# State-space networks: the gate's network first for all tokens, its exponentials and factor beside the other three, scan factors fetched by halves of the images

## The chip, the cores and the metric

The kernel runs on one core of a Trainium2 chip. The core has a matrix engine (TensorE, PE in the rows), a vector engine (VectorE, DVE), an engine for activation functions (ScalarE, ACT), a general one (GpSimd, POOL), a queue that issues transfers (SyncE, SP), and 16 DMA engines. Each engine works through its own list of instructions in order and is held up by waits on semaphores. The metric is device time in microseconds for one execution of the whole program; lower is better.

## What is computed

A vision tower on 32 images of 3 x 128 x 128. A tokenizer makes 65 tokens of 192 numbers for each image (2080 tokens in all). Two attention blocks follow, a mixture of experts, then a state-space layer, then a gated mixture of experts. The change is in the state-space layer alone. Cut to what matters, it computes, for every image, token by token:

```
def _mlp(x, w1, b1, w2, b2):
    return jax.nn.silu(x @ w1 + b1) @ w2 + b2

A_log = -jnp.abs(_mlp(x, A_w1, A_b1, A_w2, A_b2))       # 16 numbers a token
Bv = _mlp(x, B_w1, B_b1, B_w2, B_b2)                    # 16
Cv = _mlp(x, C_w1, C_b1, C_w2, C_b2)                    # 16
delta = jax.nn.sigmoid(_mlp(x, d_w1, d_b1, d_w2, d_b2)) # 192
dt = jnp.exp(log_dt)

def step(state, inp):
    a, b, c, dlt, u_t = inp
    dA = jnp.exp(a[:, None, :] * dt[None, :, None])
    cur = u_t[:, :, None] * (b[:, None, :] * dt[None, :, None])
    state = (dlt[:, :, None] * state + (1.0 - dlt[:, :, None]) * cur) * dA
    y = jnp.sum(state * c[:, None, :], axis=2) + u_t * D_param
    return (state, y)
```

The hidden layers of A, B and C have 384 units, that of the gate (d) has 192. The kernel doesn't form the sigmoid. It keeps exp(-z) of the gate's output z, called the ratio: the input of the scan is the gain G = ratio times dt times u, and the logarithm of 1 + ratio goes into the exponent of the scan's factor.

## The kernel before, in words

`state_space` has three stages, each a block that all engines enter and leave together: a block ends when the last engine has come to its end.

**The stage of the networks** (names `ssm_mlp_*`). The tokens are normalised and turned into columns `xT` (96 rows, 2 halves). SP loads the weights. Then the tokens are taken in 8 groups of 4 images, 260 columns each. For every group TensorE computes 11 tiles of hidden units (L2024): 9 of 128 rows for A, B and C, and 2 of 96 rows for the gate. Tile n goes to PSUM bank n mod 4, and TensorE may start it once ScalarE has emptied tile n - 4 (the wait of L2021, `s_act` at n - 3). ScalarE empties each with a Silu into `hid` (L2066). One group later follows the second layer, `layer2(g - 1)`: 9 matmuls for B, C and A into bank 4 (L2007) and 4 for the gate into banks 5 and 6 (L2013). ScalarE then empties them in `evacuate2(g - 1)`: B and C into `BC` (L2050), A into `ST` (L2052), the gate's output into `ratio` (L2056).

After the eighth group, VectorE clamps `ratio` (L1985), ScalarE takes its exponential (L2073, two instructions of 96 x 2080, one for each half of the 192 channels), VectorE makes the gain `G` (L1988), and ScalarE writes log(1 + ratio) into `ST` (L2076). SP, at the end of its list, waits for the last group (L1932), writes `BC` to DRAM (`bandc`, L1934), reads it back spread over 128 rows into `brep` and `crep` (L1937), writes `G` to DRAM (`gains`, L1940) and waits until that has landed (L1941). Then the block ends.

**The scan** (names `ssm_scan_*`) has 48 units of 128 rows (8 channels by 16 states) and 1056 columns (16 images of 66 columns): units 0 to 23 for the first half of the images, 24 to 47 for the second. In each unit SP fetches the gains spread over the rows (`grep`, L2113), TensorE makes the exponents from `ST` (L2168), ScalarE their exponential (L2156), VectorE the product with `brep` (L2137) and the scan itself (L2144), GpSimd the product with `crep` (L2127), and TensorE sums over the states (L2181). VectorE and GpSimd wait for both of `brep` and `crep` before the first unit (L2122, L2131).

**The last stage** turns the result back and adds it to the rows.

What sets the order is the code itself: each engine's list is written out by hand, and only semaphores tie them. An activation function needs its table on ScalarE; where the next function is in another one, the compiler puts an `ACT_TABLE_LOAD` ahead of it.

Of the kernel before, what the change touches and what calls it, by code (L numbers as in the profile page):

```python
# [1849 lines left out]
def state_space(nc, name, rows, known, stats, gains, bandc, w, fetch):  # L1850
# [3 lines left out]
    NL1 = 11  # L1854
# [14 lines left out]
    with ExitStack() as ctx:  # L1869
# [8 lines left out]
        s_rep = st.sem("rep")  # L1878
        with ExitStack() as ctx2:  # L1879
# [12 lines left out]
            hid = [s2.sbuf(f"hid{p}", [PARTS, NL1, GROUP]) for p in range(2)]  # L1892
            BC = s2.sbuf("BC", [32 + STATE, COLS])
# [5 lines left out]
            s_w, s_l1, s_act, s_l2, s_e2, s_sc, s_dt, s_c, s_edge, s_one, s_dtr, s_sel, s_exp, s_cl, s_ln, s_gain, s_skip = (  # L1899
                s2.sem(n) for n in ("w", "l1", "act", "l2", "e2", "sc", "dt", "c", "edge", "one", "dtr", "sel", "exp", "cl", "ln", "gain", "skip"))  # L1900
            block = ctx2.enter_context(nc.Block())
            NB2, NL2 = 5, 5
# [4 lines left out]
            def _(sp):  # L1907
# [52 lines left out]
            def _(dve):  # L1960
# [22 lines left out]
                dve.wait_ge(s_e2, NB2 * groups)  # L1983
# [12 lines left out]
            def _(pe):  # L1996
# [5 lines left out]
                def layer2(g):  # L2002
                    pe.wait_ge(s_act, NL1 * (g + 1))
                    wait(pe, s_e2, NB2 * g)
                    for k in range(3):
                        for i, (_, slot, ft) in enumerate(slots):
                            last = nc.tensor.matmul(ps[32 * slot:32 * slot + STATE, 4 * BANK:4 * BANK + GROUP], W2[:, i, k, :], hid[g % 2][:, ft + k, :],  # L2007
                                                    start=(k == 0), stop=(k == 2))
                            if k == 2:
                                last.then_inc(s_l2, 1)  # L2010
                    for mb in range(2):
                        for kb in range(2):
                            last = nc.tensor.matmul(ps[0:HALF, (5 + mb) * BANK:(5 + mb) * BANK + GROUP], W2d[:, kb, HALF * mb:HALF * mb + HALF],  # L2013
                                                    hid[g % 2][0:HALF, 9 + kb, :], start=(kb == 0), stop=(kb == 1))
                        last.then_inc(s_l2, 1)

                for g in range(groups):
                    for ft in range(NL1):
                        c0, rows_ = l1(ft)
                        n = NL1 * g + ft  # L2020
                        wait(pe, s_act, n - 3)  # L2021
                        for kb in range(2):
                            k = HALF + kb
                            last = nc.tensor.matmul(ps[0:rows_, (n % 4) * BANK:(n % 4) * BANK + GROUP], W1[0:k, kb, c0:c0 + rows_],  # L2024
                                                    xT[0:k, kb, GROUP * g:GROUP * g + GROUP], start=(kb == 0), stop=(kb == 1))
                        last.then_inc(s_l1, 1)
                    if g >= 1:
                        layer2(g - 1)
# [3 lines left out]
            def _(act):  # L2032
# [5 lines left out]
                act.wait_ge(s_edge, 4)  # L2038

                def evacuate2(g):  # L2040
# [13 lines left out]
                    for mb in range(2):  # L2054
                        act.wait_ge(s_l2, NL2 * g + 4 + mb)
                        nc.scalar.activation(ratio[:, mb, GROUP * g:GROUP * (g + 1)], ps[0:HALF, (5 + mb) * BANK:(5 + mb) * BANK + GROUP], ACT.Identity,  # L2056
                                             bias=b2d[:, mb:mb + 1]).then_inc(s_e2, 1)

                for g in range(groups):
                    for ft in range(NL1):  # L2060
                        _, rows_ = l1(ft)
                        n = NL1 * g + ft
# [3 lines left out]
                        nc.scalar.activation(hid[g % 2][0:rows_, ft, :], ps[0:rows_, (n % 4) * BANK:(n % 4) * BANK + GROUP],  # L2066
                                             ACT.Silu).then_inc(s_act, 1)
# [6 lines left out]
                for kb in range(2):  # L2074
                    act.wait_ge(s_exp, kb + 1)
                    nc.scalar.activation(tokens(ST[0:HALF, kb, :]), ratio[:, kb, :].rearrange("p (i c) -> p i c", c=SEQ), ACT.Ln, bias=1.0).then_inc(s_ln, 1)  # L2076


        with ExitStack() as ctx2:
# [50 lines left out]
            def _(dve):  # L2130
                dve.wait_ge(s_rep, 32)  # L2131

                def inputs(n):
                    _, _, cols = unit(n)
# [791 lines left out]
```

## Time and profile before

| | us |
|---|---|
| median of 3 runs | 1965.28 |
| lowest and highest | 1960.82, 1969.39 |
| the profiled execution, its own time | 1966.56 |
| its span in the trace | 1964.8 |
| TensorE busy | 1634.4 (83%) |
| VectorE busy | 1070.3 (54%) |
| ScalarE busy | 774.4 (39%) |
| GpSimd busy | 737.5 (38%) |
| mean granted clock of TensorE | 0.893 of full speed |
| the networks' first matmul | at 1414.1 |
| the scan's first matmul | at 1542.9 |
| the last stage's first matmul | at 1729.6 |

Times inside the trace count from the start of the span. The stage of the networks takes about 129 us of matmuls and tail, the scan about 187 us. The granted clock has two levels: 1.0 is 2.4 GHz and 0.5 is 1.2 GHz. A busy share over the whole span says little on a change of this kind: what counts is which engine is waited for in the networks' stage, and what ends last at its border to the scan.

### The profile page before, as it was taken

Reading aid. Unit: us, or ns where it says so; the run is one execution under the profiler, and the core shown is the slowest. Engines: PE = TensorE matmul, PEld = TensorE weight load, DVE = VectorE, ACT = ScalarE, POOL = GpSimd, SP = SyncE. Lnnn points to the kernel's source line nnn. Section 1 sums busy time; section 2 is a strip of 40 time slices with the busy share of each in tenths; the row PEclk is TensorE's granted clock in tenths of the full one; section 3 lists DMA queues with packets and bytes.
Section 4 is the critical chain, followed back from the end, with each engine's and each line's share of the span. In section 5 each row is a group of like instructions: output and inputs, shape, how many; then the busy total and the mean of one; then the engine's idle time right before and its main releaser. Section 6 shows DMA issues by size and latency. Waiting matters only on the chain. (4 is left out here: it accounts for less than half of the span.)

```text
span 1964.8 us, 34671 instructions
## 1 busy us (share of the span) xinstructions
PE 1634.4 (83%) x11223; PEld 1272.7 (65%) x11224; DVE 1070.3 (54%) x3226; ACT 774.4 (39%) x1433; POOL 737.5 (38%) x680
## 2 busy tenths in 40 slices
PE   3889999959999948887988889996399477767997
PEld 2657777748888834775677879996276233366564
DVE  2678988856667514387276512121700599942332
ACT  0557777723555521372254421111355332324100
POOL 2556767621222204142433023332200399920232
PEclk9989999979999958797988779998599699957999
DMA  3244343323333122000000645552600766534110
GB/s 64 41 94 83 71 81 78 74 65 94 112 109 110 42 67 62 1 3 13 1 2 18 178 122 148 156 157 62 137 1 0 182 158 160 143 87 128 41 47 28
DMA packets 219419, 158.14 MB, mean 80 GB/s; under 512 B 116583, under 2 KB 196404, under 8 KB 218794
## 3 DMA queue, kind: packets, MB, share of 16 engines
q1 hardware_dynamic: 206405, 141.18, 29.2%
q0 software_dynamic: 6528, 14.19, 2.5%
q10 hardware_dynamic: 6374, 1.33, 0.4%
q8 instruction: 64, 1.05, 0.2%
q14 instruction: 48, 0.39, 0.1%
HBM read 106.05 MB, written 32.35 MB: 70 GB/s over the span
## 5 line engine op out<-in xcount | busy, mean ns | idle before, releaser
L2127 POOL TENSOR_TENSOR ssm_scan_prod<-ssm_scan_S,ssm_crep 128x1056 f32<-128x1056 f32 x48 | 159.4, 3320 | 146.0 <-DVE ssm_scan_S L2144 146.0
L1259 PE MATMUL a_psum<-a2w_W,a_hT 128*128 128x256 f32 (+1 forms) x640 | 150.9, 383 | 5.4 <-DVE a_z L1060 4.5
L755 PE MATMUL a_psum<-a_W,a_hT 126*128 126x256 f32 x512 | 135.6, 398 | 0.0
L1259 PEld LDWEIGHTS a_psum<-a2w_W,a_hT 128*128 128x128 f32 (+1 forms) x640 | 119.9, 192 | 21.2 <-issue 6.6
L2168 PE MATMUL ssm_scan_psum<-ssm_ST,ssm_EW 112*128 112x512 f32 (+1 forms) x288 | 106.8, 509 | 23.9 <-PEq L1879 21.3
L2698 PE MATMUL moe_tiles_psum<-moe_tiles_XT,moe_tiles_mine 96*128 96x128 f32 x960 | 119.1, 281 | 2.0 <-DMA moe_tiles_mine<-moe_W 2.0
L2698 PEld LDWEIGHTS moe_tiles_psum<-moe_tiles_XT,moe_tiles_mine 96*128 96x128 f32 x960 | 113.3, 195 | 5.1 <-DMA moe_tiles_mine<-moe_W 2.5
L2144 DVE TENSOR_TENSOR_SCAN ssm_scan_S<-ssm_scan_X,ssm_scan_psum 128x1056 f32<-128x1056 f32 x48 | 113.0, 2354 | 4.7 <-ACT ssm_scan_psum L2156 0.4
L2168 PEld LDWEIGHTS ssm_scan_psum<-ssm_ST,ssm_EW 112*128 112x128 f32 x288 | 52.8, 197 | 92.8 <-issue 71.6
L755 PEld LDWEIGHTS a_psum<-a_W,a_hT 126*128 126x128 f32 x512 | 91.3, 193 | 30.8 <-issue 21.8
L543 POOL TENSOR_TENSOR a_rstd<-a_rstd,a_mhalf 128x8 f32<-128x8 f32 x64 | 105.2, 1643 | 5.0
L2745 ACT ACTIVATE moe_tiles_GT<-moe_tiles_psum 128x512 f32<-128x512 f32 x80 | 39.1, 491 | 161.7 <-PE moe_tiles_psum L2698 123.4
L2790 DVE TENSOR_TENSOR moe_tiles_Y<-moe_tiles_psum,moe_B 128x192 f32<-128x192 f32 x40 | 14.3, 358 | 157.4 <-PE moe_tiles_psum L2682 157.4
L2156 ACT ACTIVATE ssm_scan_psum<-ssm_scan_psum 128x1056 f32<-128x1056 f32 x48 | 49.7, 1035 | 120.7 <-PE ssm_scan_psum L2168 120.7
L2725 PE MATMUL glu_tiles_psum<-glu_W,glu_tiles_XT 96*128 x192 | 84.3, 583 | 6.4 <-DVE glu_tiles_XT L2775 5.5
L2653 POOL DMA_INDIRECT ys<-moe_tiles_Y,moe_target x40 | 39.6, 990 | 129.9 <-DVE moe_tiles_Y L2790 123.6
L2682 PE MATMUL moe_tiles_psum<-moe_W,moe_tiles_GT 128*128 x480 | 84.5, 326 | 0.0
L2024 PE MATMUL ssm_mlp_psum<-ssm_mlp_xT,ssm_mlp_W 96*128 96x260 f32 (+3 forms) x352 | 80.7, 389 | 2.6 <-SPq L1930 2.6
L1017 POOL TENSOR_TENSOR a_yb<-a_y,a2w_b 128x256 f32<-128x256 f32 x16 | 11.6, 726 | 179.6 <-DVE a_O L1106 167.8
L563 POOL TENSOR_TENSOR a_yb<-a_y,a_b 128x512 f32<-128x512 f32 x32 | 40.8, 1276 | 96.9 <-DVE a_O L638 96.9
L2682 PEld LDWEIGHTS moe_tiles_psum<-moe_W,moe_tiles_GT 128*128 128x128 f32 x480 | 77.1, 190 | 0.0
L2024 PEld LDWEIGHTS ssm_mlp_psum<-ssm_mlp_xT,ssm_mlp_W 96*128 96x128 f32 (+3 forms) x352 | 66.2, 188 | 16.0 <-issue 2.9
(640 smaller groups left out, 3906.6 us busy)
## 6 DMA issues: line engine op xcount, KB each, us to landing
ssm_scan_grep<-gains SPq DMA_DIRECT2D x48, 528.0 KB, 4.7
moe_tiles_mine<-moe_W SPq DMA_DIRECT2D x40, 576.0 KB
a2w_X<-t SPq DMA_DIRECT2D x192, 96.0 KB
t<-a_O SPq DMA_DIRECT2D x128, 64.0 KB
xrows<-in_x SPq DMA_DIRECT2D x30, 192.0 KB
a_X<-xrows SPq DMA_DIRECT2D x60, 91.9 KB, 3.0
a_PX<-t SPq DMA_DIRECT2D x96, 48.0 KB
moe_raw_first<-in_L_ffn_w SPq DMA_DIRECT2D x8, 576.0 KB
```

Of the source, the lines that this page charges most:

```text
L543: nc.gpsimd.tensor_tensor(out[:], out[:], mhalf[:], ALU.pow).then_inc(s[done], 1)
L563: nc.gpsimd.tensor_tensor(yb[:], y[:], spread(b2[:], 1, tiles), ALU.add).then_inc(s["yb"], 1)
L755: last = nc.tensor.matmul(KQ[q][:, j, :], hT[0:MAIN, q, PARTS * j:PARTS * j + PARTS], W[0:MAIN, :], start=False, stop=True)
L1259: last = nc.tensor.matmul(KQ[:, j, :], hT[i % 2][0:rows, k, PARTS * j:PARTS * j + PARTS], W[0:rows, k, :], start=(k == 0), stop=(k == 4))
L2024: last = nc.tensor.matmul(ps[0:rows_, (n % 4) * BANK:(n % 4) * BANK + GROUP], W1[0:k, kb, c0:c0 + rows_], xT[0:k, kb, GROUP * g:GROUP * g ...
L2127: nc.gpsimd.tensor_tensor(prod[n % 2][:], S[n % 2][:], crep[:, cols], ALU.mult).then_inc(s_prod, 1)
L2144: nc.vector.tensor_tensor_scan(S[n % 2][:], X[n % 2][:], E[n % 2], 0.0, ALU.add, ALU.mult).then_inc(s_scan, 1)
L2156: nc.scalar.activation(E[n % 2], E[n % 2], ACT.Exp).then_inc(s_coef, 1)
L2168: last = nc.tensor.matmul(E[n % 2][:, a:b], EW[:, j, :], ST[:, j // (NCH // 2), HCOLS * h + a:HCOLS * h + b], start=True, stop=True)
L2682: last = nc.tensor.matmul(made(p), GT[p][0:w_, f, :], W2[0:w_, f, bass.ds(e, 1), :].rearrange("p a c -> p (a c)"), start=(f == 0), stop=(f ...
L2698: last = nc.tensor.matmul(hidT(1 - p, f, 1), mine[q][0:HALF + kb, kb, PARTS * f:PARTS * f + PARTS], XT[1 - p][0:HALF + kb, kb, :], start=( ...
L2725: last = nc.tensor.matmul(hid(c), XT[p][0:k, kb, :], W1[0:k, kb, bass.ds(e, 1), cut * c:cut * c + cut].rearrange("p a c -> p (a c)"), star ...
```

## The change

The gate's network is taken out of the groups. TensorE and ScalarE first go through all 8 groups with the gate's 2 hidden tiles alone, in buffers of their own (`hidd`), with the gate's second layer one group behind (`layer2d`, `evacuate2d`); its last call comes after the second tile of the main loop. The main loop has 9 tiles in a group instead of 11, and a second layer without the gate. VectorE clamps and forms `G` while the main loop runs. ScalarE does the two exponentials behind groups 1 and 2 of the main loop and the two logarithms behind groups 4 and 5 (`BEHIND`), between the emptying of one group's second layer and the first Silu of the next group. SP writes `gains` first, and then `bandc`, `brep` and `crep` in two halves of the images, the first when groups 0 to 3 are done. The waits of VectorE and GpSimd in the scan are made for each half. The number of matmuls, of activations and of bytes moved is as before.

```diff
-    NL1 = 11
+    NL1 = 9
...
+            BEHIND = {1: ("exp", 0), 2: ("exp", 1), 4: ("ln", 0), 5: ("ln", 1)}
...
-                sp.wait_ge(s_e2, NB2 * groups)
-                for i in range(2):
-                    sp.dma_start(dram(bandc, i * STATE * COLS, [(COLS, STATE), (1, COLS)]), BC[32 * i:32 * i + STATE, :]).then_inc(s_sc, 16)
-                sp.wait_ge(s_sc, 32)
-                for i, rep in enumerate((brep, crep)):
-                    sp.dma_start(rep[:], dram(bandc, i * STATE * COLS, [(COLS, STATE), (0, 8), (1, COLS)])).then_inc(s_rep, 16)
                 for kb in range(2):
                     sp.wait_ge(s_gain, kb + 1)
-                    sp.dma_start(dram(gains, kb * HALF * COLS, [(COLS, HALF), (1, COLS)]), G[:, kb, :]).then_inc(s_sc, 16)
-                sp.wait_ge(s_sc, 64)
+                    sp.dma_start(dram(gains, kb * HALF * COLS, [(COLS, HALF), (1, COLS)]), G[:, kb, :]).then_inc(s_gs, 16)
+                for h in range(2):
+                    sp.wait_ge(s_e2, NB2 * (groups // 2) * (h + 1))
+                    for i in range(2):
+                        sp.dma_start(dram(bandc, i * STATE * COLS + HCOLS * h, [(COLS, STATE), (1, HCOLS)]),
+                                     BC[32 * i:32 * i + STATE, HCOLS * h:HCOLS * h + HCOLS]).then_inc(s_sc, 16)
+                    sp.wait_ge(s_sc, 32 * (h + 1))
+                    for i, rep in enumerate((brep, crep)):
+                        sp.dma_start(rep[:, HCOLS * h:HCOLS * h + HCOLS],
+                                     dram(bandc, i * STATE * COLS + HCOLS * h, [(COLS, STATE), (0, 8), (1, HCOLS)])).then_inc(s_rep[h], 16)
+                sp.wait_ge(s_gs, 32)
...
+                def layer2d(g):
+                    pe.wait_ge(s_act, 2 * (g + 1))
+                    wait(pe, s_ed, NLD * g)
...
+                for g in range(groups):
+                    for j in range(2):
+                        first(2 * g + j, g, NL1 + j)
+                    if g >= 1:
+                        layer2d(g - 1)
                 for g in range(groups):
                     for ft in range(NL1):
...
+                        first(2 * groups + NL1 * g + ft, g, ft)
+                        if g == 0 and ft == 1:
+                            layer2d(groups - 1)
                     if g >= 1:
                         layer2(g - 1)
...
+                def exponential(kb):
+                    act.wait_ge(s_cl, kb + 1)
+                    nc.scalar.activation(ratio[:, kb, :], ratio[:, kb, :], ACT.Exp, scale=-1.0).then_inc(s_exp, 1)
+
+                def logarithm(kb):
+                    act.wait_ge(s_exp, kb + 1)
+                    nc.scalar.activation(tokens(ST[0:HALF, kb, :]), ratio[:, kb, :].rearrange("p (i c) -> p i c", c=SEQ), ACT.Ln, bias=1.0).then_inc(s_ln, 1)
...
                     if g >= 1:
                         evacuate2(g - 1)
+                    if g in BEHIND:
+                        kind, kb = BEHIND[g]
+                        (exponential if kind == "exp" else logarithm)(kb)
                 evacuate2(groups - 1)
-                for kb in range(2):
-                    act.wait_ge(s_cl, kb + 1)
-                    nc.scalar.activation(ratio[:, kb, :], ratio[:, kb, :], ACT.Exp, scale=-1.0).then_inc(s_exp, 1)
-                for kb in range(2):
-                    act.wait_ge(s_exp, kb + 1)
-                    nc.scalar.activation(tokens(ST[0:HALF, kb, :]), ratio[:, kb, :].rearrange("p (i c) -> p i c", c=SEQ), ACT.Ln, bias=1.0).then_inc(s_ln, 1)
...
-                pool.wait_ge(s_rep, 32)
                 for n in range(UNITS):
-                    _, _, cols = unit(n)
+                    h, j, cols = unit(n)
+                    if j == 0:
+                        pool.wait_ge(s_rep[h], 32)
```

ScalarE's list at the end of the networks' stage, before: the last group's outputs, then the exponentials and the logarithms, each pair with one table load.

```order
L2050 ACTIVATE ssm_mlp_BC<-ssm_mlp_psum,ssm_mlp_b 16x4x65 x2
L2052 ACTIVATE ssm_ST<-ssm_mlp_psum,ssm_mlp_b 16x2x4x65
L2056 ACTIVATE ssm_mlp_ratio<-ssm_mlp_psum,ssm_mlp_b2d 96x260 x2
L2073 ACT_TABLE_LOAD
L2073 ACTIVATE ssm_mlp_ratio<-ssm_mlp_ratio 96x2080 x2
L2076 ACT_TABLE_LOAD
L2076 ACTIVATE ssm_ST<-ssm_mlp_ratio 96x32x65 x2
```

They are gone from there. ScalarE's list in the changed kernel around the first exponential, behind group 1 of the main loop (`hid` is what the Silu writes; L2103 is the Silu, L2081 the exponential):

```order
L2103 ACTIVATE ssm_mlp_hid<-ssm_mlp_psum 128x260 x15
L2074 ACTIVATE ssm_mlp_BC<-ssm_mlp_psum,ssm_mlp_b 16x4x65 x2
L2076 ACTIVATE ssm_ST<-ssm_mlp_psum,ssm_mlp_b 16x2x4x65
L2081 ACT_TABLE_LOAD
L2081 ACTIVATE ssm_mlp_ratio<-ssm_mlp_ratio 96x2080
L2103 ACT_TABLE_LOAD
L2103 ACTIVATE ssm_mlp_hid<-ssm_mlp_psum 128x260 x9
```

One large activation now stands between two table loads, ahead of the nine Silus of group 2; the same pattern stands there four times.

SP's list from the last weights to the end of the stage, before:

```order
L1934 DMA bandc<-ssm_mlp_BC 16x2112 x2
L1937 DMA ssm_brep<-bandc 128x1x2112
L1937 DMA ssm_crep<-bandc 128x1x2112
L1940 DMA gains<-ssm_mlp_G 96x2112 x2
L1879 UNCONDITIONAL_BRANCH
```

And the same piece of SP's list in the changed kernel:

```order
L1937 DMA gains<-ssm_mlp_G 96x2112 x2
L1941 DMA bandc<-ssm_mlp_BC 16x1056 x2
L1945 DMA ssm_brep<-bandc 128x1x1056
L1945 DMA ssm_crep<-bandc 128x1x1056
L1941 DMA bandc<-ssm_mlp_BC 16x1056 x2
L1945 DMA ssm_brep<-bandc 128x1x1056
L1945 DMA ssm_crep<-bandc 128x1x1056
L1879 UNCONDITIONAL_BRANCH
```

The write of `gains` has moved from the end to the front, and only the second half of `brep` and `crep` stands last, with no wait for it ahead of the branch that leaves the block.

## Rows read from the trace of the kernel before

**Rows 1.** Timeline, the last full group; start us, us, engine, line, instructions, [idle before].

```profile
1500.86 1.50 PE L2007 MATMUL ssm_mlp_psum<-ssm_mlp_hid,ssm_mlp_W 128*16 128x260 f32 x18
...
1502.29 1.99 PE L2013 MATMUL ssm_mlp_psum<-ssm_mlp_hid,ssm_mlp_W2d 96*96 96x260 f32 x8
1502.47 0.96 ACT L2050 ACTIVATE ssm_mlp_BC<-ssm_mlp_psum,ssm_mlp_b 16x260 f32<-16x260 f32 x2 [1.12 <-PE ssm_mlp_psum L2007]
1503.46 0.69 ACT L2052 ACTIVATE ssm_ST<-ssm_mlp_psum,ssm_mlp_b 16x520 f32<-16x520 f32 x1
...
1504.12 9.85 PE L2024 MATMUL ssm_mlp_psum<-ssm_mlp_xT,ssm_mlp_W 96*128 96x260 f32 x44
...
1506.08 0.39 ACT L2066 ACTIVATE ssm_mlp_hid<-ssm_mlp_psum 128x260 f32<-128x260 f32 x1 [0.49 <-PE ssm_mlp_psum L2024]
```

**Rows 2.** Timeline, from the last tile of the networks to the scan's first unit.

```profile
1513.89 1.50 PE L2007 MATMUL ssm_mlp_psum<-ssm_mlp_hid,ssm_mlp_W 128*16 128x260 f32 x18
...
1518.19 1.50 PE L2007 MATMUL ssm_mlp_psum<-ssm_mlp_hid,ssm_mlp_W 128*16 128x260 f32 x18 [0.87 <-ACT ssm_mlp_ratio L2056]
...
1519.79 0.97 ACT L2050 ACTIVATE ssm_mlp_BC<-ssm_mlp_psum,ssm_mlp_b 16x260 f32<-16x260 f32 x2 [1.74 <-PE ssm_mlp_psum L2007]
1520.78 0.69 ACT L2052 ACTIVATE ssm_ST<-ssm_mlp_psum,ssm_mlp_b 16x520 f32<-16x520 f32 x1
...
1522.35 1.28 ACT L2073 ACT_TABLE_LOAD   x1
1522.36 0.77 SPq L1934 DMA_DIRECT2D bandc<-ssm_mlp_BC  x2
...
1523.74 3.76 ACT L2073 ACTIVATE ssm_mlp_ratio<-ssm_mlp_ratio 96x2080 f32<-96x2080 f32 x2
...
1526.24 0.58 SPq L1937 DMA_DIRECT2D ssm_brep<-bandc  x1
1526.86 0.60 SPq L1937 DMA_DIRECT2D ssm_crep<-bandc  x1
1527.52 1.28 ACT L2076 ACT_TABLE_LOAD   x1
1528.12 2.61 SPq L1940 DMA_DIRECT2D gains<-ssm_mlp_G  x2
1528.81 3.76 ACT L2076 ACTIVATE ssm_ST<-ssm_mlp_ratio 96x2080 f32<-96x2080 f32 x2
...
1542.88 6.56 PE L2168 MATMUL ssm_scan_psum<-ssm_ST,ssm_EW 112*128 112x512 f32 x12 [21.26 <-PEq L1879]
...
1548.35 1.26 DVE L2137 TENSOR_TENSOR ssm_scan_X<-ssm_scan_grep,ssm_brep 128x1056 f32<-128x1056 f32 x1 [17.96 <-DMA ssm_scan_grep<-gains]
...
1549.71 2.35 DVE L2144 TENSOR_TENSOR_SCAN ssm_scan_S<-ssm_scan_X,ssm_scan_psum 128x1056 f32<-128x1056 f32 x1
```

**Rows 3.** What SP's queue waited for, 1500 to 1560; us, times, longest.

```profile
SPq L1879 <- DMA gains<-ssm_mlp_G: 11.7, 1, 11.7
```

**Rows 4.** Windows of TensorE; stretch, length, busy (matmuls), granted clock, DMA share, GB/s.

```profile
73.40:76.80 3.40, 1.77 (x13) 1.00 0.53 81
76.80:80.20 3.40, 3.40 (x11) 0.50 0.02 5
80.20:83.60 3.40, 3.40 (x34) 0.99 0.02 5
...
1548.00:1551.40 3.40, 1.44 (x5) 1.00 0.92 216
1551.40:1554.80 3.40, 2.69 (x3) 0.50 0.74 174
1554.80:1558.20 3.40, 3.40 (x14) 0.50 0.52 139
...
1517.30:1520.70 3.40, 2.53 (x24) 1.00 0.00 0
```

**Rows 5.** Windows, all engines; stretch, length, busy of PE, PEld, DVE, ACT, POOL, clock, DMA share, GB/s.

```profile
1530.40:1542.60 12.20, 0.00 (x0) 0.00 (x0) 0.00 (x0) 2.17 (x2) 0.00 (x0) 0.50 0.89 255
```

More of the change, by code:

```diff
@@ L1877, in state_space @@
         yT = st.sbuf("yT", [HALF, 2, TOKENS])
-        s_rep = st.sem("rep")
+        s_rep = [st.sem(f"rep{h}") for h in range(2)]
         with ExitStack() as ctx2:
@@ L1892, in state_space @@
             hid = [s2.sbuf(f"hid{p}", [PARTS, NL1, GROUP]) for p in range(2)]
+            hidd = [s2.sbuf(f"hidd{p}", [HALF, 2, GROUP]) for p in range(2)]
             BC = s2.sbuf("BC", [32 + STATE, COLS])
@@ L2013, in layer2, with first @@
                             last = nc.tensor.matmul(ps[0:HALF, (5 + mb) * BANK:(5 + mb) * BANK + GROUP], W2d[:, kb, HALF * mb:HALF * mb + HALF],
[L2014 to L2015 removed]
+                                                    hidd[g % 2][:, kb, :], start=(kb == 0), stop=(kb == 1))
+                        last.then_inc(s_l2d, 1)
+                def first(n, g, ft):
+                    c0, rows_ = l1(ft)
+                    wait(pe, s_act, n - 3)
+                    for kb in range(2):
+                        k = HALF + kb
+                        last = nc.tensor.matmul(ps[0:rows_, (n % 4) * BANK:(n % 4) * BANK + GROUP], W1[0:k, kb, c0:c0 + rows_],
+                                                xT[0:k, kb, GROUP * g:GROUP * g + GROUP], start=(kb == 0), stop=(kb == 1))
+                    last.then_inc(s_l1, 1)
+                for g in range(groups):
[3 more added lines that the diff above has]
+                        layer2d(g - 1)
                 for g in range(groups):
                     for ft in range(NL1):
[L2019 to L2026 removed]
+                        first(2 * groups + NL1 * g + ft, g, ft)
+                        if g == 0 and ft == 1:
+                            layer2d(groups - 1)
                     if g >= 1:
@@ L2037, in _, with evacuate2d @@
                 nc.scalar.activation(dtr[HALF:HALF + STATE, :], dtr[HALF:HALF + STATE, :], ACT.Exp).then_inc(s_dt, 1)
-                act.wait_ge(s_edge, 4)
+                def evacuate2d(g):
+                    for mb in range(2):
+                        act.wait_ge(s_l2d, NLD * g + mb + 1)
+                        nc.scalar.activation(ratio[:, mb, GROUP * g:GROUP * (g + 1)], ps[0:HALF, (5 + mb) * BANK:(5 + mb) * BANK + GROUP], ACT.Identity,
+                                             bias=b2d[:, mb:mb + 1]).then_inc(s_ed, 1)
                 def evacuate2(g):
@@ L2053, in evacuate2 @@
                                                  ACT.Abs, bias=b2[p, 0:1]).then_inc(s_e2, 1)
[L2054 to L2057, printed above, removed]
+                def exponential(kb):
[4 more added lines that the diff above has]
+                    nc.scalar.activation(tokens(ST[0:HALF, kb, :]), ratio[:, kb, :].rearrange("p (i c) -> p i c", c=SEQ), ACT.Ln, bias=1.0).then_inc(s_ln, 1)
+                for g in range(groups):
+                    for j in range(2):
+                        n = 2 * g + j
+                        act.wait_ge(s_l1, n + 1)
+                        if g >= 2 and j == 0:
+                            act.wait_ge(s_l2d, NLD * (g - 1))
+                        nc.scalar.activation(hidd[g % 2][:, j, :], ps[0:HALF, (n % 4) * BANK:(n % 4) * BANK + GROUP], ACT.Silu).then_inc(s_act, 1)
+                    if g >= 1:
+                        evacuate2d(g - 1)
+                act.wait_ge(s_edge, 4)
                 for g in range(groups):
                     for ft in range(NL1):
-                        _, rows_ = l1(ft)
-                        n = NL1 * g + ft
+                        n = 2 * groups + NL1 * g + ft
                         act.wait_ge(s_l1, n + 1)
```

22 lines of the change are left out of this document (12 added, 10 removed).

## The prediction

> **What bounds the kernel now.** The chain of waits on the page belongs to the last experts and does not reach this layer, so I read timelines. In the networks' stage [rows 1] TensorE's rows follow each other without a hole while ScalarE sits idle 0.49 us ahead of each 0.39 us Silu: TensorE bounds the stage. A group costs 13.03 us, from 1500.86 to 1513.89: 1.43 for the second layer of B, C and A (to 1502.29), 1.83 for the gate's (to 1504.12) and 9.77 for 11 tiles, 0.888 each. At the border to the scan [rows 2] TensorE stands still for 21.26 us. In that hole the reader is to see a chain: the last outputs end at 1521.47 (A) and 1522.3 (the gate), SP writes `bandc` at 1522.36, `brep` and `crep` are issued at 1526.24 and 1526.86, `gains` from 1528.12, and SP then waits 11.7 us for `gains` to land [rows 3]. DMA moves 255 GB/s meanwhile [rows 5]. So what ends last is a transfer queued behind 2.1 MB of spread copies. The scan starts at 1542.88, 28.99 us after the last tile's end at 1513.89; its first scan instruction at 1549.71.
>
> **Part 1, the gate's second layer moves ahead.** Of its 8 pieces, 6 stood ahead of the last tile before, 2 behind it. Now all 8 are ahead: 2 x 1.83 = +3.7 us until the last tile. The tiles are the same 88. The two gate tiles of a group and 1.83 us of `layer2d` fit ScalarE's 2 x 0.39 + 0.84 us easily, so nothing waits in that first loop. That ScalarE no longer waits for GpSimd's borders ahead of the first Silu costs and gains nothing, as TensorE bounds there.
>
> **Part 2, four large activations inside the main loop.** This is the step on which the result hangs. Count from S, the start of a group's second layer on TensorE. ScalarE begins to empty it at S + 1.6 and is done at S + 3.3 (1504.15 - 1500.86) [rows 1]. Before, Silu followed. Now comes a table load and a large Exp (first load 1522.35, Exp 1523.74, so 1.39), the Exp itself 3.76 / 2 = 1.88, then the load back to Silu's table, 1.29 (1527.52 to 1528.81) [rows 2], and a Silu of 0.39. That ends at S + 8.3. TensorE is through with the second layer at S + 1.43 and may start 4 tiles, since tile n needs tile n - 4 emptied: 4 x 0.888, to S + 4.98. The fifth waits for the first Silu, until S + 8.3. **A hole of 3.3 us, four times, +13.2 us.** ScalarE's idle half doesn't hide it, because the slack is spread in pieces of 0.49 us and only four banks of lead stand between the engines. Afterwards TensorE runs on without further holes, at its own 0.888 a tile. Both ends: 2.7 us a hole, if a load overlaps the end of the work ahead, makes +10.8; 3.9 makes +15.6.
>
> **Part 3, the clock.** In [rows 4] TensorE was idle 1.6 us between 73.4 and 76.8; the granted clock was then 0.5 (1.2 GHz) for 3.4 us and came back to 1.0 (2.4 GHz). It was idle 2.0 us between 1548.0 and 1551.4, and the clock was 0.5 for 6.8 us, though TensorE worked. After 0.9 us idle, in the stretch from 1517.3, I see no fall that belongs to it. A hole of 3.3 us is longer than both that brought a fall, so I take it that each of the four brings one, of 3.4 or of 6.8 us. Half of that time is lost to TensorE: 1.7 or up to 3.4 us; mean 2.35 (part of the longer fall lies in the hole itself). Nothing but TensorE bounds there, so it is lost in full: 4 x 2.35 = **+9.4 us**, between 0 (no fall) and +13.6.
>
> On this the Trainium skill (TensorE: Matmul & The Clock Gate, "Why this matters for your kernels") warns of idle gaps between bursts of matmuls, after which the clock falls back. The rows agree, with falls after 1.6 and 2.0 us of idleness.
>
> The Trainium skill (ScalarE: Activation LUTs, "Rules for kernel authors") advises to do all work of one table set before switching; the change does the opposite, 8 switches in place of 2. Its section "What ACT_TABLE_LOAD costs" adds 1.38 us of drain to each 1.28 us load, by which this sum would be 11 us longer. The trace disagrees on the drain: the second Exp ends at 1527.50 and its successor's load stands at 1527.52.
>
> **Part 4, the border.** Counted from the last tile's end, T. The second layer of group 6 is emptied at T + 3.3, and group 7's waits for that: its start is at T + 3.4. From there [rows 2] 1.60 until ScalarE begins (1518.19 to 1519.79) and 1.68 until A is out (1521.47): T + 6.7. `bandc` and its landing take 3.9 (1522.36 to 1526.24), with half the bytes hardly less, as 0.26 MB are 1 us at 255 GB/s: I keep 3.9 and have T + 10.6. Two issues of 0.6 us bring SP to T + 11.8. Leaving the block took 0.45 us (2.61 of issue from 1528.12 and 11.7 of wait end at 1542.43; the scan began at 1542.88). **The scan starts at T + 12.3 instead of T + 29.0: -16.7 us.** `gains` has long landed by then: it is ready in group 3 and has several groups for its landing.
>
> **Part 5, the scan's first fetch.** Before, `grep` came 5.4 us after the scan's start (1548.35 against 1542.88), with a free queue. Now the second half of `brep` and `crep`, 1.08 MB or 4.2 us at 255 GB/s, was issued 1.7 us earlier and is ahead of it: +2.5, less some overlap. I take **+2.0**, between +0.5 (they interleave well) and +4.5 (the copies take their whole time first and share it with the next fetches). The wait for halves lets units 0 to 23 go on without it.
>
> **Sum:** 3.7 + 13.2 + 9.4 - 16.7 + 2.0 = **+11.6 us**. The profiled execution took 1966.56 us, 1.76 more than its span of 1964.8; it would come to 1978.2. It lies 1.3 us above the median of the three runs, 1965.28, and on that median the same sum gives **1977 us**, +0.6%. With all low ends (clock 0, holes 10.8, fetch 0.5) it is -1.7 us, 1964; with all high ends (13.6, 15.6, 4.5) it is +20.7 us, 1986.
>
> **Rivals.**
> *The clock holds.* The holes are there, but TensorE works at full speed after them. 3.7 + 13.2 - 16.7 + 2.0 = +2.2 us: 1967 to 1968. For it: the lead of four queued tiles makes each hole's neighbourhood dense, and the scan at 2.5 of 3.4 us busy keeps full clock. Against: the two falls in [rows 4]. Chance 0.25.
> *Faster: the activations are hidden.* If the load and the large activation overlap TensorE's lead almost wholly, a hole is under 0.6 us, and no clock falls: 3.7 + 2.4 - 16.7 + 2.0 = -8.6; wholly hidden -11.0: 1954 to 1957. The point from which it decides is ScalarE's time from the second layer's last output to the next Silu's end: 5.0 us against TensorE's lead, and holes vanish at 1.7 us for that stretch, while the rows give 5.0. Chance 0.06.
> *The border is not shortened as counted.* If the copies of the second half hold up the scan's first fetch or the leaving of the block by a further 5 us (they are 1.08 MB without a wait ahead of the branch), the sum is +17: 1982. The wait that goes is then replaced by the fetch's own. Chance 0.10.
> *A switch of tables costs more amid short activations.* If each of the 8 loads cost twice its 1.28 us, the holes would be 2.6 us longer, 4 x 2.6 = +10.2 us: 1987. The point from which it decides is any gap ahead of a load; the rows show 0.02 us between the second Exp's end (1527.50) and the load (1527.52), and Ln at 1528.81. The skill's drain, above, would be such a cost. Chance 0.02.
> That leaves 0.57 for the forecast, its own range 1972 to 1983.
>
> **Chances and range.** A measurement of this kernel can tell about 0.5% from no change, that is 9.8 us: slower is above 1975.1. The forecast's 1977 is near that line, so a third of its chance (one clock stretch a hole instead of two, or shorter holes) falls into "same". Faster: 0.06 (the second rival, and no other). Same: 0.25 + 0.16 = 0.41. Slower: 0.41 + 0.10 + 0.02 = 0.53. The range from 1964 to 1986 leaves out the hidden case and the drain.
>
> **What would show it.** In the changed kernel's timeline, each large activation (L2081, L2085) between two table loads, and behind each a row of TensorE that was idle about 3.3 us until a Silu; four of them. In windows, the granted clock at 0.5 for 3 to 7 us behind each. The time from the stage's first matmul to its last tile grows by some 26 us. At the border TensorE's hole falls from 21 us to about 7, SP's wait for `gains` at the block's end is gone, and the first scan instruction comes about 8.8 us after the scan's start instead of 6.8. The prediction is wrong if the holes are shorter than 2 us, if the clock stays at 1.0 behind them, or if the scan's first fetch takes over 10 us.

## The result: slower by 0.4%, and the profile after

| | before | after |
|---|---|---|
| median, us (20 runs each) | 1963.77 | 1973.44 |
| ratio after to before | | 1.0042, 95% interval 1.0029 to 1.0056 |
| span of the profiled execution | 1964.8 | 1975.8 |
| networks' first matmul to their last tile's end | 99.78 | 125.28 |
| from there to the scan's first matmul | 28.99 | 11.16 |
| from that matmul to the first scan instruction | 6.83 | 9.16 |
| sum of these three | 135.60 | 145.60 |
| first scan instruction to the last stage | 179.85 | 180.08 |

The last tile's end is taken where the next second layer starts (1513.89 and 1536.03), and the "first scan instruction" is VectorE's first `TENSOR_TENSOR_SCAN`. The two medians lie 9.7 us apart; the ratio, estimated from all the runs, is 1.0042 with its interval.

The forecast was 1977 us and +0.6%, with a range from 1964 to 1986; 1973.44 lies in it. It also lies below 1975.1, from which the prediction counted "slower": by its own line this is its "same", to which it gave 0.41 against 0.53. The interval of the ratio is clear of 1 all the same. On the trace the three parts that the change touches add up to +10.0 us; the forecast's sum was +11.6. The rest of the difference between the two spans lies in stages that the change doesn't touch.

Timeline of the changed kernel around the first large activation; start us, us, engine, line, instructions, [idle before]. It answers to [rows 1], where a Silu followed at once.

```profile
1457.00 1.50 PE L2013 MATMUL ssm_mlp_psum<-ssm_mlp_hid,ssm_mlp_W 128*16 128x260 f32 x18
...
1458.43 3.79 PE L2032 MATMUL ssm_mlp_psum<-ssm_mlp_xT,ssm_mlp_W 96*128 96x260 f32 x16
...
1459.60 0.69 ACT L2076 ACTIVATE ssm_ST<-ssm_mlp_psum,ssm_mlp_b 16x520 f32<-16x520 f32 x1
1460.30 1.28 ACT L2081 ACT_TABLE_LOAD   x1
1461.59 1.94 ACT L2081 ACTIVATE ssm_mlp_ratio<-ssm_mlp_ratio 96x2080 f32<-96x2080 f32 x1
1463.55 1.28 ACT L2103 ACT_TABLE_LOAD   x1
...
1464.84 1.22 ACT L2103 ACTIVATE ssm_mlp_hid<-ssm_mlp_psum 128x260 f32<-128x260 f32 x4
...
1465.28 6.35 PE L2032 MATMUL ssm_mlp_psum<-ssm_mlp_xT,ssm_mlp_W 96*128 96x260 f32 x20 [3.07 <-ACT ssm_mlp_hid L2103]
```

The reader is to see four tiles (16 matmul rows) started at 1458.43, then TensorE idle for 3.07 us until the first Silu behind the second table load. The four Silus then run in one go, 1.22 us, as four banks lie full. The same hole stands at 1479.85, 1505.64 and 1520.20.

Windows of TensorE in the changed kernel; stretch, length, busy (matmuls), granted clock, DMA share, GB/s. The first three lie around the first hole, the next two around the second, the last two behind the third and the fourth.

```profile
1462.90:1466.30 3.40, 1.02 (x5) 1.00 0.00 0
1466.30:1469.70 3.40, 3.40 (x10) 0.50 0.78 239
1469.70:1473.10 3.40, 3.40 (x28) 0.99 0.02 5
1476.50:1479.90 3.40, 0.34 (x3) 1.00 0.00 0
1480.00:1486.80 6.80, 6.80 (x16) 0.50 0.39 119
1507.30:1510.60 3.30, 3.30 (x9) 0.50 0.52 121
1521.00:1524.30 3.30, 3.30 (x9) 0.50 0.00 0
```

Behind each hole TensorE works at 1.2 GHz, for 3.4 us behind the first, third and fourth, for 6.8 us behind the second. The starts of the second layers divide the loop into groups:

```profile
1471.56 1.50 PE L2013 MATMUL ssm_mlp_psum<-ssm_mlp_hid,ssm_mlp_W 128*16 128x260 f32 x18
1487.81 1.50 PE L2013 MATMUL ssm_mlp_psum<-ssm_mlp_hid,ssm_mlp_W 128*16 128x260 f32 x18
1497.35 1.50 PE L2013 MATMUL ssm_mlp_psum<-ssm_mlp_hid,ssm_mlp_W 128*16 128x260 f32 x18
1511.92 1.50 PE L2013 MATMUL ssm_mlp_psum<-ssm_mlp_hid,ssm_mlp_W 128*16 128x260 f32 x18
1526.48 1.50 PE L2013 MATMUL ssm_mlp_psum<-ssm_mlp_hid,ssm_mlp_W 128*16 128x260 f32 x18
```

A group of the main loop without a hole takes 9.54 us (1487.81 to 1497.35). The four with one take 14.56 (from 1457.00), 16.25, 14.57 and 14.56, together 21.8 us more. That divides without a rest. TensorE resumes 8.28 us after S, the start of the group's second layer (1457.00 to 1465.28), where its four tiles would have let it go on at S + 4.98, so a hole costs 3.30 us (its row shows 3.07 of idleness, since the fourth tile's last matmul ends 0.24 us behind the point at which the next could have begun). 9.54 + 3.30 + 1.72 for half of a 3.4 us fall is 14.56, and 9.54 + 3.30 + 3.41 for half of the 6.8 us one is 16.25. So the holes cost 13.2 us and the clock 8.6.

The border to the scan, timeline of the changed kernel; it answers to [rows 2].

```profile
1536.03 1.50 PE L2013 MATMUL ssm_mlp_psum<-ssm_mlp_hid,ssm_mlp_W 128*16 128x260 f32 x18
...
1539.46 1.50 PE L2013 MATMUL ssm_mlp_psum<-ssm_mlp_hid,ssm_mlp_W 128*16 128x260 f32 x18 [1.93 <-ACT ssm_ST L2076]
...
1542.05 0.69 ACT L2076 ACTIVATE ssm_ST<-ssm_mlp_psum,ssm_mlp_b 16x520 f32<-16x520 f32 x1
1542.76 0.78 SPq L1941 DMA_DIRECT2D bandc<-ssm_mlp_BC  x2
1545.32 0.55 SPq L1945 DMA_DIRECT2D ssm_brep<-bandc  x1
1545.91 0.59 SPq L1945 DMA_DIRECT2D ssm_crep<-bandc  x1
...
1547.19 6.24 PE L2204 MATMUL ssm_scan_psum<-ssm_ST,ssm_EW 112*128 112x512 f32 x12 [6.22 <-PEq L1879]
...
1554.99 1.26 DVE L2173 TENSOR_TENSOR ssm_scan_X<-ssm_scan_grep,ssm_brep 128x1056 f32<-128x1056 f32 x1 [74.48 <-DMA ssm_scan_grep<-gains]
1556.35 2.35 DVE L2180 TENSOR_TENSOR_SCAN ssm_scan_S<-ssm_scan_X,ssm_scan_psum 128x1056 f32<-128x1056 f32 x1
```

The hole of 21.26 us is down to 6.22, and SP's wait of [rows 3] has no row any more. The border did what the change promised. The first gains come 7.8 us after the scan's start, where they came after 5.5.

### The profile page after: what moved, and what is told of

Read it like the earlier page. It is cut to its first block and busy times, and to the rows that moved or that the text cites. A ratio compares the mean times of both kernels' runs of the same rounds, so it can differ in the third digit from the quotient of the medians.

```text
span 1975.8 us, 34694 instructions
## 1 busy us (share of the span) xinstructions
PE 1641.7 (83%) x11223; PEld 1279.0 (65%) x11224; DVE 1070.8 (54%) x3226; ACT 781.8 (40%) x1439; POOL 736.9 (37%) x680
## 5 line engine op out<-in xcount | busy, mean ns | idle before, releaser
L2032 PE MATMUL ssm_mlp_psum<-ssm_mlp_xT,ssm_mlp_W 97*128 97x260 f32 (+3 forms) x352 | 92.2, 421 | 14.3 <-ACT ssm_mlp_hid L2103 12.3
L2173 DVE TENSOR_TENSOR ssm_scan_X<-ssm_scan_grep,ssm_brep 128x1056 f32<-128x1056 f32 x48 | 59.2, 1233 | 74.5 <-DMA ssm_scan_grep<-gains 74.5
L2032 PEld LDWEIGHTS ssm_mlp_psum<-ssm_mlp_xT,ssm_mlp_W 97*128 97x128 f32 (+3 forms) x352 | 71.0, 204 | 34.2 <-ACT ssm_mlp_hid L2103 13.9
L2689 POOL DMA_INDIRECT ys<-moe_tiles_Y,moe_target x40 | 39.5, 987 | 130.6 <-DVE moe_tiles_Y L2826 127.7
L1017 POOL TENSOR_TENSOR a_yb<-a_y,a2w_b 128x256 f32<-128x256 f32 x16 | 11.6, 726 | 178.1 <-DVE a_O L1106 166.4
```

Of the source, the lines that this page charges most:

```text
L2173: nc.vector.tensor_tensor(X[n % 2][:], grep[n % NEWEST][:], brep[:, cols], ALU.mult).then_inc(s_x, 1)
```

## Experiments

The theory has five terms: the gate's second layer ahead of the last tile (+3.7 us), holes (+13.2), clock (+8.6), border (-17.8), and the copies ahead of the first fetch (+2.3). Each run has the kernel before beside it on its own chip, one chip for the first four and another for the last four; seven banks and combined have 6 runs, the others 12, the kernel before 29 on each chip. "Stage" below is the time in the trace from the networks' first matmul to the first scan instruction: 135.6 us before, 145.6 after.

| run | ratio to before, 95% interval | to last tile | to scan | to first scan instruction | stage |
|---|---|---|---|---|---|
| before | 1 | 99.8 | 29.0 | 6.8 | 135.6 |
| after, again | 1.0031 (1.0010 to 1.0052) | 125.8 | 11.2 | 8.8 | 145.7 |
| seven banks | 0.9951 (0.9932 to 0.9970) | 107.0 | 11.2 | 8.7 | 126.9 |
| holes filled | 1.0000 (0.9982 to 1.0018) | 116.7 | 11.2 | 9.1 | 137.0 |
| late exponentials | 0.9985 (0.9969 to 1.0002) | 103.7 | 20.6 | 6.2 | 130.6 |
| second halves in the scan | 1.0018 (1.0000 to 1.0037) | 125.4 | 9.7 | 6.2 | 141.3 |
| one hole | 0.9990 (0.9966 to 1.0015) | 117.3 | 11.2 | 9.0 | 137.4 |
| combined | 0.9912 (0.9885 to 0.9940) | 106.6 | 6.3 | 6.2 | 119.1 |
| halves alone | 0.9970 (0.9949 to 0.9990) | 99.7 | 22.0 | 7.1 | 128.8 |

The columns of times come from one profiled execution of each kernel. One part of them is scatter: in every profile the stage begins at 0.5 of the clock, and for how long differs, from 3.8 us (halves alone) over 4.4 (after) to 5.7 (after, again), which, at half the speed, is worth up to 1 us in the first column. Windows of TensorE, after and after again:

```profile
1410.75:1415.10 4.35, 4.35 (x10) 0.50 1.06 230
1422.52:1428.10 5.58, 5.58 (x13) 0.50 0.89 190
```

Differences between groups inside the loop are free of this, and are used below where a size hangs on it.

### The changed kernel again

> The changed kernel again, to stand beside the others on the same chip. Expected as measured: ratio to the kernel before 1.003 to 1.006, four holes of TensorE of 3.07 us in the networks' main loop, a fall of the granted clock behind each.

Ratio 1.0031, interval 1.0010 to 1.0052. Four holes of 3.07 us each, with falls of 3.4, 3.4, 3.4 and 6.8 us; the long one is behind the fourth hole here, not the second. So the hole repeats from execution to execution, and which fall is long doesn't.

### Does the lead of four tiles make the holes? Seven banks

Banks 5, 6 and 7 are free in the main loop but for one call of the gate's second layer.

```diff
+            def bank(n):
+                m = n - 2 * groups
+                return (n % 4 if m < 0 else (0, 1, 2, 3, 7, 5, 6)[m % 7]) * BANK
...
-                    wait(pe, s_act, n - 3)
+                    m = n - 2 * groups
+                    if m in (5, 6):
+                        pe.wait_ge(s_ed, NLD * groups)
+                    wait(pe, s_act, n - 3 if m < 4 else n - 6)
```

> The changed kernel with seven PSUM banks for the main loop's tiles in place of four (banks 5, 6 and 7 join), so that TensorE may run seven tiles ahead of ScalarE. Theory (the holes come from a lead of four tiles against 5 us of ScalarE's work on loads and one large activation, and the clock falls because of the holes): the lead grows by 3 x 0.888 = 2.66 us, each hole shrinks from 3.07 to about 0.6 us (it resumed at S + 8.28, and seven tiles end at S + 1.43 + 6.2 = 7.65), no clock falls behind them; 9.8 us of holes and 9.5 us of clock go, -19 us against the changed kernel, ratio to before 0.994 to 0.996. Rival (the holes cost, but the clock falls for another reason, such as the load itself or the phase of the stage): only 9.8 us go, ratio about 0.999 to 1.000, and the falls stay. Rival (the lost time lies elsewhere): ratio stays at 1.004.

Measured: the holes are 0.43 us, and the clock stays at 1.0. Timeline of TensorE, the first group with a large activation, and windows of TensorE, both of this run:

```profile
1460.10 1.50 PE L2017 MATMUL ssm_mlp_psum<-ssm_mlp_hid,ssm_mlp_W 128*16 128x260 f32 x18
1461.54 6.43 PE L2040 MATMUL ssm_mlp_psum<-ssm_mlp_xT,ssm_mlp_W 96*128 96x260 f32 x28
1468.39 2.03 PE L2040 MATMUL ssm_mlp_psum<-ssm_mlp_xT,ssm_mlp_W 96*128 96x260 f32 x8 [0.43 <-ACT ssm_mlp_hid L2111]
1470.34 1.50 PE L2017 MATMUL ssm_mlp_psum<-ssm_mlp_hid,ssm_mlp_W 128*16 128x260 f32 x18
```

```profile
1455.00:1520.00 65.00, 63.29 (x348) 1.00 0.16 45
```

Seven tiles (28 rows) instead of four stand ahead of the hole. ScalarE's list is the same, with the same eight loads. The stage is 18.9 us shorter than the changed kernel's in the run beside it (145.7 to 126.9), against 19 expected, and the ratio of 0.9951 is below that of the kernel before. What the loads and the large activations cost is set by the lead: with four tiles against 5 us of ScalarE's work they cost TensorE 21.8 us, with seven tiles 2.8, since a group with a large activation takes 10.24 us (1460.10 to 1470.34) in place of 9.54, four times 0.7. The rival by which only 9.8 us go, because the clock falls from the loads or the phase of the stage, falls: all eight loads are still there.

### How much of it is the clock? Holes filled with matmuls

```diff
+                        if ft == 4 and g - 1 in BEHIND:
+                            for _ in range(7):
+                                nc.tensor.matmul(ps[:, 7 * BANK:7 * BANK + GROUP], W1[0:HALF, 0, 0:PARTS],
+                                                 xT[0:HALF, 0, GROUP * g:GROUP * g + GROUP], start=True, stop=True)
                         first(2 * groups + NL1 * g + ft, g, ft)
```

> The changed kernel with seven matmuls of 96 x 128 x 260 added ahead of the fifth tile behind each large activation; nothing reads their result, so they add 4 x 3.1 us of TensorE's work that lies in the holes. Theory (the clock's fall comes from the hole): TensorE's stand turns into work, the clock stays at 1.0 through the main loop, and 9.5 us go against the changed kernel; ratio to before 0.999 to 1.001. Rival (the slow stretch behind the hole isn't the clock's, or the clock falls anyway): no gain, ratio 1.004 or a little above, since the added work can stick out of the holes by 0.1 us each.

The added matmuls run just where the hole was (L2045), the fifth tile starts at S + 8.29 (1464.02, with S at 1455.73) as in the changed kernel (1465.28 - 1457.00 = 8.28). Timeline of TensorE and a window that begins with the first large activation and ends behind the last, of this run:

```profile
1455.73 1.50 PE L2013 MATMUL ssm_mlp_psum<-ssm_mlp_hid,ssm_mlp_W 128*16 128x260 f32 x18
1457.16 3.79 PE L2032 MATMUL ssm_mlp_psum<-ssm_mlp_xT,ssm_mlp_W 96*128 96x260 f32 x16
1460.79 3.23 PE L2045 MATMUL ssm_mlp_psum<-ssm_mlp_xT,ssm_mlp_W 96*128 96x260 f32 x14
1464.02 4.67 PE L2032 MATMUL ssm_mlp_psum<-ssm_mlp_xT,ssm_mlp_W 96*128 96x260 f32 x20
1468.61 1.50 PE L2013 MATMUL ssm_mlp_psum<-ssm_mlp_hid,ssm_mlp_W 128*16 128x260 f32 x18
```

```profile
1455.00:1525.00 70.00, 70.00 (x379) 1.00 0.15 41
```

For the same piece the changed kernel's window shows 0.89 of the clock:

```profile
1457.00:1536.00 79.00, 66.73 (x325) 0.89 0.14 37
```

With work whose result nobody reads the kernel gets 8.8 us faster in the stage (145.74 to 136.95), against 9.5 expected. In the loop only the clock can have given that, since the fifth tile starts no earlier. A group with a hole takes 12.88 us here (1455.73 to 1468.61) where it took 14.56, or 16.25 with the long fall; over the four groups that is 8.4 us less than in the changed kernel's profile, beside the 8.6 us worked out above. The expectation of 9.5 had put 4 x 0.24 us to the clock that belong to the holes.

### The early exponentials undone

```diff
-            BEHIND = {1: ("exp", 0), 2: ("exp", 1), 4: ("ln", 0), 5: ("ln", 1)}
+            BEHIND = {}
...
                 evacuate2(groups - 1)
+                for kb in range(2):
+                    exponential(kb)
+                for kb in range(2):
+                    logarithm(kb)
```

SP writes `gains` behind the second halves again.

> One part undone: exponentials and logarithms stand behind the last group again as in the kernel before (two table loads, no switch in the main loop), and SP writes gains last; the gate's network stays first, and brep and crep stay in halves. Theory: no holes and no falls in the main loop (-21.8 us against the changed kernel), but the scan starts about 23.5 us after the last tile in place of 11.2, with a free queue for its first fetch (-2.3), so +12.3 - 2.3 = +10 back: about -11.8 us against the changed kernel, ratio to before 0.998 to 1.000. Rival (the border's saving was what the halves and the gate's early network give, not the early exponentials): the scan starts 14 us or less after the last tile, ratio 0.993. Rival (the gate's network first costs more than 2 x 1.83 us): the last tile ends more than 104.5 us after the stage's first matmul, ratio above 1.001.

The last tile ends 103.67 us after the first matmul, 3.9 more than before: that is the price of the gate's network going first, against 3.7 predicted, and no more than that. The scan starts 20.6 us after it, 3 us earlier than expected. Timeline of this run:

```profile
1521.27 0.77 SPq L1938 DMA_DIRECT2D bandc<-ssm_mlp_BC  x2
1522.56 3.76 ACT L2081 ACTIVATE ssm_mlp_ratio<-ssm_mlp_ratio 96x2080 f32<-96x2080 f32 x2
1524.04 0.55 SPq L1942 DMA_DIRECT2D ssm_brep<-bandc  x1
...
1526.93 2.61 SPq L1946 DMA_DIRECT2D gains<-ssm_mlp_G  x2
...
1535.18 5.63 PE L2208 MATMUL ssm_scan_psum<-ssm_ST,ssm_EW 112*128 112x512 f32 x12 [15.70 <-PEq L1879]
```

From the last issue of `gains` (1529.54) to the scan's start are 5.6 us, where it was 12.2 before (1530.73 to 1542.88, [rows 2]). So with half the copies ahead the gains land in less than half the time (the expectation had put them later), though not as fast as the 4.4 us that they took in the changed kernel with nothing ahead. The stage is 130.6 us, 5.0 less than before and 15.2 less than the changed kernel, where 11.8 less was expected. The ratio, 0.9985, isn't clear of 1, but its interval is clear of the changed kernel's. Both rivals fall, since the scan doesn't start within 14 us of the last tile, and the last tile comes before 104.5 us. The early exponentials, the core of the change, cost more than they brought: at the border they save 9.5 us (20.6 to 11.2), give back 2.5 at the first fetch (6.2 to 8.8), and cost 22.2 in the loop (103.7 to 125.8).

### The halves alone

The kernel before, with `brep` and `crep` in halves and nothing else.

```diff
-                sp.wait_ge(s_e2, NB2 * groups)
-                for i in range(2):
-                    sp.dma_start(dram(bandc, i * STATE * COLS, [(COLS, STATE), (1, COLS)]), BC[32 * i:32 * i + STATE, :]).then_inc(s_sc, 16)
+                for h in range(2):
+                    sp.wait_ge(s_e2, NB2 * (groups // 2) * (h + 1))
...
```

> The kernel before with one part of the change alone: brep and crep in two halves of the images, the first when groups 0 to 3 are done; the gate's network, the exponentials and the gains stay where they were. Theory (the gains' landing is late because 2.16 MB is queued ahead): with 1.08 MB ahead and a shorter landing of bandc the scan starts 22 to 24 us after the last tile in place of 29.0, nothing else moves, -5 to -7 us; ratio to before 0.9965 to 0.9975. Rival (the gains' own 1.6 MB and its landing take the time whatever is ahead): 27 us or more, ratio above 0.999.

Ratio 0.9970, interval 0.9949 to 0.9990; the scan starts 22.0 us after the last tile. What SP's queue waited for in this run, against 11.7 us in [rows 3]:

```profile
SPq L1879 <- DMA gains<-ssm_mlp_G: 4.7, 1, 4.7
```

So the smallest part of the change brings 7.0 of the border's 17.8 us and has no cost in the loop. It confirms the reading of [rows 2]: the gains were late because of what was queued ahead of them. SP issues the gains 14.2 us behind the last tile in both kernels (1528.12 - 1513.89, and 1522.83 - 1508.62 here); only their landing is shorter. Two things changed for it together, half the bytes ahead and copies issued 1.2 us earlier behind the last tile (1519.77 - 1508.62 = 11.15 us against 12.35) thanks to the shorter landing of `bandc`; how the 7.0 us divide between them isn't shown.

### The copies ahead of the first fetch

```diff
+                    if n in (6, 9):
+                        rep, i = (brep, 0) if n == 6 else (crep, 1)
+                        sp.dma_start(rep[:, HCOLS:2 * HCOLS], dram(bandc, i * STATE * COLS + HCOLS, [(COLS, STATE), (0, 8), (1, HCOLS)])).then_inc(s_rep[1], 16)
```

> The changed kernel, with the fetch of the second halves of brep and crep moved into the scan: SP issues them behind the gains of units 6 and 9 (they are needed at unit 24), so that nothing is queued ahead of the first fetch. Theory (the first scan instruction stands 2.3 us later behind the scan's start than before because 1.08 MB is ahead of its gains): it comes 6.2 to 6.9 us after the scan's start in place of 9.2, and the scan starts 1.2 us earlier for the two issues that are gone; -3.5 us against the changed kernel, from the stage's first matmul to the first scan instruction 142 us, ratio to before 1.001 to 1.003. Rival (the slow clock at the scan's start is what delays it): still 8.7 to 9.2 us after the start, only -1.2 us. Rival (the copies in the scan disturb it): the scan takes more than 181 us from its first scan instruction to the last stage's first matmul, where the others have 179.8 to 180.6.

The first scan instruction comes 6.2 us after the scan's start (1547.44), in place of 9.2, and the scan starts 1.4 us earlier. The clock at the start is at 0.5 as in the changed kernel, so it isn't what delays it:

```profile
1546.70:1553.30 6.60, 5.86 (x9) 0.50 0.71 169
```

From the first scan instruction to the last stage are 179.5 us, so the copies inside the scan disturb nothing. The ratio moves from 1.0031 to 1.0018, which is inside the intervals and between two chips; what shows the effect is the trace, 145.6 to 141.3 us.

### One long hole

```diff
-            BEHIND = {1: ("exp", 0), 2: ("exp", 1), 4: ("ln", 0), 5: ("ln", 1)}
+            BEHIND = {3}
...
                     if g in BEHIND:
-                        kind, kb = BEHIND[g]
-                        (exponential if kind == "exp" else logarithm)(kb)
+                        for kb in range(2):
+                            exponential(kb)
+                        for kb in range(2):
+                            logarithm(kb)
```

> The changed kernel with both exponentials and both logarithms behind group 3, in one piece: three table loads in place of eight, four large activations in a row. Theory: one hole of 3.07 + 2 x 1.28 less 1.28 ... worked out: ScalarE's piece is 3 x 1.28 + 4 x 1.94 = 11.6 us in place of 4.5, so the hole is 3.07 + 7.1 = 10.2 us, and one fall of the clock costs 1.7 to 3.4; together about 12.8 us in place of 21.8, so -9 us against the changed kernel; from the first matmul to the last tile 116 to 117 us; ratio to before 0.998 to 1.000. Rival (what counts is only the hole's length and the clock costs more after a long one): the hole is as above, the falls last longer than 7 us behind it, and the ratio is above 1.001.

One hole of 9.97 us, and the clock was at 0.5 from 1486.7 to 1500.4. TensorE worked 6.30 us of that:

```profile
1486.70:1500.40 13.70, 6.30 (x15) 0.50 0.38 118
```

The rest of the fall lies in the hole and costs nothing. The last tile comes 117.3 us after the first matmul (116 to 117 expected), and the ratio is 0.9990, not clear of 1. Against the changed kernel the stage is 8.3 us shorter (145.7 to 137.4).

The Trainium skill (ScalarE: Activation LUTs, "Rules for kernel authors") advises to group work by table set and to do all of one set before switching. The trace agrees, with these 8.3 us, though the larger part of them is the clock's. The holes together shrink by 3.0 us, from 13.2 to 10.2 (9.97 and the 0.24 from above): five loads fewer take 6.4 us from ScalarE's work, and against that TensorE's lead hides a piece once in place of four times. The rest is the clock: half of 6.30 us is 3.15, where it was 8.6. Its fall is paid once, and partly lies in the hole. The rival with a clock dearer behind a long hole falls.

### Combined

Seven banks, the second halves in the scan, `BC` kept beyond the stage so that SP needn't wait there for its second landing, and the last second layer in bank 0.

```diff
+        BC = st.sbuf("BC", [32 + STATE, COLS])
...
+                    if h == 1:
+                        break
                     sp.wait_ge(s_sc, 32 * (h + 1))
...
+            def out2(g):
+                return (4 if g < groups - 1 else 0) * BANK
```

> The seven banks of e2, and three edits at the border: the last second layer goes to bank 0, which is empty by then, and needn't wait for the emptying of the one ahead; the second halves are fetched in the scan as in e5; BC outlives the stage, so that SP needn't wait in the stage until its second half has landed. Theory: against e2 the scan starts 4.9 us earlier behind the last tile (1.7 for the second layer, 2.6 for the landing, 1.2 for two issues, less 0.6 that may not add up), 6.3 to 6.8 us behind it in place of 11.2, and the first scan instruction comes 2 us earlier behind the start: -7 us, first matmul to first scan instruction about 120 us; ratio to before 0.990 to 0.993. Rival (at the border something else becomes late, such as TensorE's exponents at the low clock or the first gains): -3 us or less against e2, ratio 0.994.

Timeline of this run at the border:

```profile
1516.30 2.82 PE L2024 MATMUL ssm_mlp_psum<-ssm_mlp_hid,ssm_mlp_W 128*16 128x260 f32 x36
...
1520.60 0.69 ACT L2091 ACTIVATE ssm_ST<-ssm_mlp_psum,ssm_mlp_b 16x520 f32<-16x520 f32 x1
1521.31 0.78 SPq L1942 DMA_DIRECT2D bandc<-ssm_BC  x2
...
1522.60 5.72 PE L2223 MATMUL ssm_scan_psum<-ssm_ST,ssm_EW 112*128 112x512 f32 x12 [3.48 <-PEq L1881]
```

Both second layers follow each other (36 rows), and the scan starts 6.3 us after the last tile, 4.9 earlier than with seven banks alone, as expected. Median 1946.70 against 1963.38, ratio 0.9912 with 0.9885 to 0.9940: faster than both kernels. The stage is 119.1 us, 16.5 less than before. What each of the three edits at the border brings wasn't run one by one.

## The prediction, point by point

- **What bounds.** Right: TensorE in the networks' loop, the landing of `gains` at the border. The halves alone show the second by themselves.
- **Part 1, the gate's second layer ahead, +3.7.** Right: 3.9 by the run with late exponentials (103.67 against 99.78), and 3.7 is what is left of the loop's 25.5 us (125.28 - 99.78) without holes and clock.
- **Part 2, holes, +13.2.** Right: TensorE resumed at S + 8.28 where I had 8.3, and four holes cost 13.2 us. That they come from the lead is shown by the seven banks.
- **Part 3, clock, +9.4.** 8.6 in the profiled run, 8.4 by the groups of the filled holes. The mechanism is right, and the size came close by two slips that offset each other. Falls of 3.4 and 6.8 us came 3 to 1, where I had weighed them evenly (evenly, four whole falls cost 10.2 us; 3 to 1 they cost 8.5). And I took 0.8 off because part of a fall would lie in its hole, while all four began 0.1 to 1.6 us behind it (the first hole ends at 1465.28, the fall begins at 1466.3). That the two nearly cancel is luck. The rival in which the clock holds falls with this. My reading of [rows 4] was loose as well: the idle 2.0 us from 1548.0 are the end of a stand of 2.68 us, and the 1.6 us from 73.4 are two stands, 1.31 and 0.32. And a stand of 1.93 us ahead of the changed kernel's last second layer (to 1539.46) was followed by 5.3 us at full clock, of which TensorE worked 1.5, so below 3 us the rows don't say which stand brings a fall.
- **Part 4, border, -16.7.** -17.8. The mis-sized term is `bandc`: I kept 3.9 us for it with half the bytes, and it was 2.6 (1542.76 to 1545.32). Leaving the block took 0.7 us (1546.50 to 1547.19), 0.2 more than the 0.45 I had.
- **Part 5, first fetch, +2.0.** +2.3, and shown to be the copies: without them 6.2 us.
- **Sum, +11.6.** +10.0 in the stage. The 1.6 us too many are 0.8 of the clock and 1.1 of the border, less 0.3 of the first fetch. In whole executions it is +9.7 us between the medians, +8.2 by the ratio of 1.0042. Of the 3.5 us between 1977 and 1973.44 another 1.5 come from the base: the median of three runs was 1965.28, that of twenty 1963.77.
- **Chances.** A third of 0.57 is 0.19, where I moved 0.16 to "same". "Slower" was the likelier of the two for me, and the measured time lies 1.7 us on the other side of the line (1973.44 against 1975.1).
- **No drain at table loads.** The Trainium skill (ScalarE: Activation LUTs, "What ACT_TABLE_LOAD costs") states 1.38 us of drain beside the 1.28 us load. The changed kernel's rows show none: the activation ahead of the load ends at 1460.29, the load stands at 1460.30 and the next activation at 1461.59. The rival of dearer switches falls.
- **Faster, since the activations are hidden.** Not with four banks. With seven, whose lead nearly covers the 5 us, a hole costs 0.7 us and the stage is 8.7 us shorter than before (135.6 to 126.9); the rival had 8.6 for holes under 0.6 us.

What is open: why one fall of the clock in four is longer, what decides between 0.43 and 3.07 us of standing whether a fall comes, and whether anything outside the stage has moved. In the profiled pair the networks' first matmul came 3.4 us earlier after, and what follows the scan took 4.1 us more. In the ten profiles here that first matmul stands between 1409.0 and 1422.5 us, with the same code ahead of it, so I take both for scatter; no run tests it.

## What to carry to other kernels

An engine that is idle about half the time, as ScalarE is here, can't take a long piece of work for free: what hides it is the lead that the buffers give the bounding engine, here 4 tiles of 0.888 us against 5 us. Count the lead first, and deepen it before moving work in. A hole in TensorE's work costs its own length and then the slow clock behind it, here two thirds as much again. And look at what is queued ahead of the transfer that ends last: fetching the copies ahead of it in two halves brought 7 us with no other edit.

## What the runs showed of the hardware

- A write of 16 rows to DRAM and its landing took 3.88 us with 8448 B a row and 2.56 us with 4224 B. The difference of 1.3 us is more than the 0.5 us that the 0.135 MB fewer make at 255 GB/s (before and after, two writes each).
- TensorE kept to 0.5 for 3.4 us in nine cases and 6.8 us in three, behind the same hole of 3.07 us (after, after again, second halves in the scan); a hole of 0.43 us brought no fall in eight places (seven banks, combined), and one of 9.97 us brought a fall that began inside it and lasted 13.7 us.
- The gains (two writes of 0.81 MB) landed 4.4 us after their issue with nothing ahead, 5.2 us behind 1.08 MB of copies, and 12.2 us behind 2.16 MB (after, halves alone, before).
- A table load took 1.28 us, and the activation behind it began 1.29 to 1.30 us after the load's start, with no further gap (after, eight loads in the loop).
